# A mixture of experts behind a graph layer: the order of one step's four stages on TensorE and ScalarE turned round, and half of the last reads issued by ScalarE

## The chip, the cores and the metric

The kernel runs on one core of a Trainium2 chip. The metric is the device time of one execution in microseconds (us). Five engines work side by side, each through its own list of instructions in order: TensorE (PE, matmuls and transposes; its weight loads are PEld), VectorE (DVE), ScalarE (ACT), GpSimd (POOL) and SyncE (SP), which here does nothing but issue transfers. They wait for one another by semaphores. Sixteen DMA engines move data between memory (DRAM) and the on-chip buffers.

## The reference

The input is 3327 nodes with 128 features and a signed 3327x3327 matrix. A graph layer (a GRU cell over a graph sum, and one over three attention heads) is added to the nodes. Then comes a layer of 8 experts, and it is this part that the change touches:

```python
xn = (x - mu) * rsqrt(var + EPS) * gamma + beta
logits = einsum('bsd,de->bse', xn, Wr) + br
top_vals, top_idx = top_k(logits, 2)
w = softmax(top_vals)                      # two experts for each node
for e in range(8):
    h = gelu(einsum('bsd,dh->bsh', xn, W1[e]) + b1[e])     # 128 -> 256
    y_e = einsum('bsh,hd->bsd', h, W2[e]) + b2[e]          # 256 -> 128
    y = y + y_e * w_full[..., e, None]
```

The output is the nodes plus y.

## The kernel before, in words

The nodes are padded to 3328 = 26 tiles of 128. Everything up to about 870 us is the graph layer, the router and the sorting of rows, and the change does not touch it. At its end each node's normed row stands twice in `sorted_dram`, in the regions of its two experts, with its weight and the place where its result belongs. What follows has two parts.

**The batches.** 33 batches (`BATCHES`) of 256 rows (`SIDES` = 2 tiles of 128), each of one expert. Batch n passes through:

- SP: `weights_read(n)` and `rows_read(n)` (L543 to L554) bring the expert's weights and the 256 rows into one of 8 buffers (semaphore `b_in`). The first 8 are issued together, the later ones as `batch_y(n - 8)` is done.
- PE `batch_turned(n)` (L1881, matmuls on L1887): two 128x128 transposes into PSUM. ACT `batch_in(n)` (L887, L892): gamma and beta, PSUM to SBUF.
- PE `batch_hidden(n)` (L1890, L1896): W1, two products of 128x256. ACT `batch_gelu(n)` (L895, L901): two GELUs; the second releases `b_act`.
- PE `batch_down(n)` (L1901, L1907): W2, it waits for `b_act`. ACT `batch_kept(n)` (L905, L910): adds b2 and releases `b_kept`.
- PE `batch_back(n)` (L1911, L1917): two transposes back, after `b_kept`. DVE `batch_y(n)` (L1520, L1526): weighs the rows, into one of 4 buffers (`NY`); it waits until the buffer's earlier scatter has landed (`b_out`).
- POOL (L631 to L637): two indirect transfers, each 128 rows of y to their places in `y_dram` (L635).

An fp32 product of one weight tile stands in the trace as two matmul instructions, so L1896 and L1907 have four for a batch; the two transposes of L1887 or L1917 have two in all. The PE loop runs over steps n = -3 to 32 and in each step does batch n+3's first stage, n+2's second, n+1's third and n's fourth, **in this order: turned, hidden, down, back**. ACT's loop does `batch_in(n+3)`, `batch_gelu(n+2)`, `batch_kept(n+1)`. The order of these calls is the engine's order: an engine that waits for a semaphore holds all that stands behind it.

**The last sums.** When all scatters have landed (four waits on `b_out`), SP issues six reads of `y_dram` (L569), three pieces (`PIECES`: 6, 9 and 11 tiles) of each node's first and second result: `y_of[0]`, `y_of[1]`. DVE waits for both reads of a piece (`c_in[q]` at 32), adds both to the nodes (L1537), and SP writes the piece out (L573). SP's order is six reads, then three writes.

Of the kernel before, what the change touches and what calls it, by code (L numbers as in the profile page):

```python
# [29 lines left out]
NP = TILES * 128  # L30
# [18 lines left out]
SIDES = 2  # L49
BATCH = SIDES * 128  # L50
BATCHES = -(-2 * NP // BATCH) + E - 1
SPARES = BATCHES * BATCH
# [6 lines left out]
NY = 4  # L59
# [72 lines left out]
def graph_layer_kernel(nc, x, x_t, adj_rows, adj_cols, diag, ident_in, sum_parts_in, level_at_in,  # L132
# [9 lines left out]
    with ctx:  # L142
# [3 lines left out]
        def sem(name):  # L146
            return ctx.enter_context(nc.semaphore(name))
# [140 lines left out]
        y_of = [heads[:, k, :].rearrange("p (t f) -> p t f", f=H) for k in range(2)]  # L288
# [62 lines left out]
        b_out = [sem(f"b_out{k}") for k in range(NY)]  # L351
        c_in, c_out, o_done = [sem(f"c_in{k}") for k in range(3)], sem("c_out"), sem("o_done")
        PIECES = ((0, 6), (6, 15), (15, TILES))
# [61 lines left out]
        def _(sp):  # L415
# [93 lines left out]
            for c, (c0, w) in enumerate(CHUNKS):  # L509
                for third, (t0, t1) in enumerate(THIRDS):  # L510
                    n = 3 * c + third
# [53 lines left out]
            for k in range(NY):  # L565
                sp.wait_ge(b_out[k], 16 * SIDES * len(range(k, BATCHES, NY)))
            for q, (t0, t1) in enumerate(PIECES):
                for k in range(2):
                    sp.dma_start(y_of[k][:, t0:t1, :], y_dram[SPARES + k * NP + t0 * 128:SPARES + k * NP + t1 * 128, :]  # L569
                                 .rearrange("(t p) f -> p t f", p=128)).then_inc(c_in[q], 16)  # L570
            for q, (t0, t1) in enumerate(PIECES):
                sp.wait_ge(c_out, q + 1)
                sp.dma_start(out[t0 * 128:t1 * 128, :].rearrange("(t p) f -> p t f", p=128), x_kept[:, t0:t1, :])\  # L573
# [68 lines left out]
        def _(act):  # L642
# [11 lines left out]
            for q in range(-(-TILES // 4)):  # L654
                n = min(4, TILES - 4 * q) * 128
# [231 lines left out]
            def batch_in(n):  # L887

                act.wait_ge(b_turned, n + 1)
                if n >= 3:  # L890
                    act.wait_ge(b_hid, n - 2)
                nc.scalar.activation(turned[:, n % 3, :], bank[n % 2][:, 0:BATCH], ACT.Identity, bias=beta_sb,  # L892
                                     scale=gamma_sb).then_inc(b_input, 1)

            def batch_gelu(n):  # L895

                act.wait_ge(b_hid, n + 1)
                if n >= 3:
                    act.wait_ge(b_down, n - 2)
                for a in range(HALVES):  # L900
                    last = nc.scalar.activation(act_h[:, n % 3, a, :], bank[2 + n % 2][:, a * BATCH:(a + 1) * BATCH], ACT.Gelu,  # L901
                                                bias=b1_of[a][:, n % NX, :])
                last.then_inc(b_act, 1)

            def batch_kept(n):  # L905

                act.wait_ge(b_down, n + 1)
                if n >= 2:
                    act.wait_ge(b_back, n - 1)
                nc.scalar.activation(y_t[:, n % 2, :], bank[4 + n % 2][:, 0:BATCH], ACT.Identity, bias=b2_of[:, n % NX, :])\  # L910
                    .then_inc(b_kept, 1)

            act.wait_ge(tables_ready, 1)
            for n in range(-3, BATCHES):
                if n + 3 < BATCHES:
                    batch_in(n + 3)
                if 0 <= n + 2 < BATCHES:
                    batch_gelu(n + 2)
                if 0 <= n + 1 < BATCHES:
                    batch_kept(n + 1)  # L920


        @block.vector
# [620 lines left out]
        def _(pe):  # L1544
# [336 lines left out]
            def batch_turned(n):  # L1881

                pe.wait_ge(b_in[n % NX], 32 * (n // NX + 1))
                if n >= 2:
                    pe.wait_ge(b_input, n - 1)
                for k in range(SIDES):
                    last = nc.tensor.transpose(bank[n % 2][:, 128 * k:128 * (k + 1)], batch[:, n % NX, k, 0:H], ident[:, :])  # L1887
                last.then_inc(b_turned, 1)

            def batch_hidden(n):  # L1890

                pe.wait_ge(b_input, n + 1)
                if n >= 2:
                    pe.wait_ge(b_act, n - 1)
                for a in range(HALVES):
                    last = nc.tensor.matmul(bank[2 + n % 2][:, a * BATCH:(a + 1) * BATCH],  # L1896
                                            w1_of[a][:, n % NX, :], turned[:, n % 3, :],
                                            start=True, stop=True)
                last.then_inc(b_hid, 1)

            def batch_down(n):  # L1901

                pe.wait_ge(b_act, n + 1)
                if n >= 2:
                    pe.wait_ge(b_kept, n - 1)
                for a in range(HALVES):
                    last = nc.tensor.matmul(bank[4 + n % 2][:, 0:BATCH], w2_of[a][:, n % NX, :], act_h[:, n % 3, a, :],  # L1907
                                            start=a == 0, stop=a == HALVES - 1)
                last.then_inc(b_down, 1)

            def batch_back(n):  # L1911

                pe.wait_ge(b_kept, n + 1)
                if n >= 2:
                    pe.wait_ge(b_y, n - 1)
                for k in range(SIDES):
                    last = nc.tensor.transpose(bank[6 + n % 2][:, 128 * k:128 * (k + 1)], y_t[:, n % 2, 128 * k:128 * (k + 1)],  # L1917
                                               ident[:, :])
                last.then_inc(b_back, 1)

            for n in range(-3, BATCHES):
                if n + 3 < BATCHES:
                    batch_turned(n + 3)
                if 0 <= n + 2 < BATCHES:
                    batch_hidden(n + 2)
                if 0 <= n + 1 < BATCHES:
                    batch_down(n + 1)
                if n >= 0:
                    batch_back(n)


# [42 lines left out]
```

## Time and profile before

| | us |
|---|---|
| median of 3 runs | 1002.87 (1000.69 to 1006.1) |
| the profiled execution | 1000.35 |
| its span, first to last instruction | 998.6 |
| busy in the span: PE / DVE / ACT / POOL | 873.4 / 694.8 / 626.8 / 143.4 |
| first transpose of the batches to the last scatter's issue | 882.17 to 974.72 |
| first read of the last sums issued to the span's end | 976.97 to 998.6 |

The profile is of one execution. All times below are from the start of its span. A row of the timeline has start, duration, engine, line and operation; in brackets how long the engine was idle before and what ended that. The chain of waits is the path that ended last, followed back from the last instruction. Ends of matmuls are modelled (a row on L1896 shows 1.03 us, while the next matmul starts 0.86 us after it), starts are not.

### The profile page before, as it was taken

The numbers are of one execution on the slowest core, as the hardware profiler recorded it, in microseconds if no ns is written. First come the engines' busy times: TensorE is split into PE (matmuls) and PEld (weight loads), VectorE is DVE, ScalarE is ACT, GpSimd is POOL, SyncE is SP. The second block draws the span as 40 slices with busy tenths as digits, with TensorE's granted clock in tenths as the row PEclk, the third lists the DMA queues.
The fourth block names the chain that finished last, engine by engine and source line by source line (L and its number), as shares of the span: only waits on it lengthen the run. The fifth ranks groups of instructions, "written<-read, shape, count | busy, mean of one in ns | idle before, by whom it ended". The sixth has DMA issues, their size and how long they took to land.

```text
span 998.6 us, 10507 instructions
## 1 busy us (share of the span) xinstructions
PE 873.4 (87%) x2787; PEld 458.1 (46%) x2787; DVE 694.8 (70%) x1306; ACT 626.8 (63%) x918; POOL 143.4 (14%) x182
## 2 busy tenths in 40 slices
PE   5999999899699999999999999999988977069940
PEld 5734343356475434444444444444454444058830
DVE  6533333352599989999999999999858788612223
ACT  0655455611499879898998998989723233148820
POOL 0000000000000000001001001001000407727770
PEclk9999999999799999999999999999999998579975
DMA  9876766420059974646646445222040001268727
GB/s 282 278 270 233 255 236 228 147 88 17 9 176 309 330 176 121 167 111 190 169 117 160 122 122 143 84 87 103 1 142 1 27 6 46 72 170 222 220 72 213
DMA packets 115735, 147.81 MB, mean 148 GB/s; under 512 B 11488, under 2 KB 66562, under 8 KB 114786
## 3 DMA queue, kind: packets, MB, share of 16 engines
q1 hardware_dynamic: 111906, 139.38, 47.5%
q0 software_dynamic: 3776, 7.79, 2.2%
q8 instruction: 24, 0.39, 0.2%
q14 instruction: 29, 0.24, 0.1%
HBM read 123.61 MB, written 23.55 MB: 147 GB/s over the span
## 4 chain that ended last, share of the span: by engine, by line
PE 36%; issue 24%; DVE 19%; POOL 7%; DMA 5%; ACT 4%; DVEq 3%; SPq 1%; ACTq 0%; POOLq 0%
PE psum L1618 15%; DVE work L1257 9%; PE psum L1735 7%; POOL sorted_dram L628 4%; PE psum L1701 4%; POOL y_dram L635 4%; DVE big L1266 3%; DMA big<-adj_cols_dram 2%; DVEq L1257 2%; PE psum L1601 1%; ACT work L803 1%; PE psum L1559 1%; DMA h_t<-x_t_dram 1%; DMA y_dram<-rows 1%; PE psum L1896 1%
## 5 line engine op out<-in xcount | busy, mean ns | idle before, releaser
L1735 PE MATMUL psum<-big,h 128*128 128x512 f32 (+1 forms) x1092 | 445.4, 569 | 16.9 <-DVE big L1266 16.8
L1735 PEld LDWEIGHTS psum<-big,h 128*128 128x128 f32 x1092 | 206.7, 192 | 254.7 <-issue 178.9
L1266 DVE TENSOR_TENSOR big<-work,big 128x1536 f32<-128x1536 f32 (+1 forms) x182 | 299.2, 1644 | 9.2 <-ACT work L803 3.7
L801 ACT ACTIVATE work<-work,shift 128x1024 f32<-128x1024 f32 (+1 forms) x182 | 197.9, 1087 | 45.4 <-DVE work L1257 42.8
L1618 PE MATMUL psum<-big,h 128*128 128x512 f32 x312 | 146.3, 612 | 0.0
L1257 DVE TENSOR_SCALAR work<-rows,h 128x512 f32<-128x512 f32 x312 | 137.3, 483 | 2.9 <-POOLq L616 2.9
L803 ACT ACTIVATE work<-work,shift 128x512 f32<-128x512 f32 (+1 forms) x182 | 123.1, 676 | 0.0
L595 POOL TENSOR_SCALAR_AFFINE_SELECT big<-big 128x128 f32<-128x128 f32 x50 | 25.1, 502 | 639.5 <-DMA big<-adj_cols_dram 637.3
L797 ACT ACTIVATE work<-rows,h 128x512 f32<-128x512 f32 x156 | 110.2, 707 | 0.0
L1618 PEld LDWEIGHTS psum<-big,h 128*128 128x128 f32 x312 | 56.6, 191 | 68.6 <-issue 67.9
L675 ACT ACTIVATE work<-big 128x2048 bf16<-128x2048 f32 (+1 forms) x42 | 75.0, 1785 | 2.7
L1014 DVE TENSOR_SCALAR rows<-big 128x2048 fp8e4<-128x2048 f32 x36 | 42.5, 1224 | 48.9 <-POOLq L608 48.7
L635 POOL DMA_INDIRECT y_dram<-rows x66 | 63.8, 967 | 35.3 <-issue 18.0
L628 POOL DMA_INDIRECT sorted_dram<-big x52 | 52.3, 1006 | 100.2 <-ACT big L868 85.6
L1526 DVE TENSOR_SCALAR rows<-psum,rows 128x128 f32<-128x128 f32 x66 | 20.1, 347 | 62.9 <-DMA y_dram<-rows 38.1
L1001 DVE TENSOR_TENSOR work<-work,psum 32x512 f32<-32x512 f32 (+1 forms) x7 | 4.5, 637 | 57.5 <-ACT work L690 57.5
L1896 PE MATMUL psum<-work,rows 128*128 128x256 f32 x132 | 35.5, 394 | 0.0
L1701 PE MATMUL psum<-rows,work 128*126 128x512 fp8e4 (+1 forms) x168 | 35.0, 364 | 0.0
L901 ACT ACTIVATE work<-psum,rows 128x256 f32<-128x256 f32 x66 | 27.7, 471 | 11.2 <-PE psum L1896 11.2
L1907 PE MATMUL psum<-work,rows 128*128 128x256 f32 x132 | 34.0, 380 | 0.0
L892 ACT ACTIVATE work<-psum,u_parts 128x256 f32<-128x256 f32 x33 | 18.6, 565 | 22.1 <-PE psum L1887 22.0
L1887 PE MATMUL psum<-ident,rows 128*128 128x128 f32 x66 | 13.5, 287 | 19.1 <-DMA rows<-sorted_dram 19.1
(256 smaller groups left out, 763.3 us busy)
## 6 DMA issues: line engine op xcount, KB each, us to landing
big<-adj_cols_dram SPq DMA_DIRECT2D x30, 2048.0 KB, 8.1
sorted_dram<-zeros SPq DMA_DIRECT2D x15, 910.0 KB, 14.2
big<-adj_cols_dram SPq DMA_DIRECT2D x9, 1024.0 KB, 7.1
big<-adj_cols_dram SPq DMA_DIRECT2D x6, 1536.0 KB, 6.5
rows<-experts_dram SPq DMA_DIRECT2D x33, 257.5 KB, 3.1
rows<-stats_dram SPq DMA_DIRECT2D x1, 4608.0 KB, 26.9
rows<-sorted_dram SPq DMA_DIRECT2D x33, 130.0 KB, 2.9
rows<-stats_dram SPq DMA_DIRECT2D x1, 3840.0 KB, 21.0
```

The source lines that it names most:

```text
L628: nc.gpsimd.indirect_dma_start(out=sorted_dram[:, :], out_offset=bass.IndirectOffsetOnAxis(ap=slot_at[:, t, k:k + 1], axis=0), in_=rows_ou ...
L635: nc.gpsimd.indirect_dma_start(out=y_dram[:, :], out_offset=bass.IndirectOffsetOnAxis(ap=where_i[:, n, k:k + 1], axis=0), in_=y_sb[:, n % ...
L675: nc.scalar.activation(unused[:, 0:t1 - t0, 0:w], cols_of(c, t0, t1), ACT.Relu, scale=-1.0, accum_out=negative[:, NQ * c + g:NQ * c + g + ...
L797: nc.scalar.activation(place, row_of(c, LAST), ACT.Relu, bias=h[:, bass.ds(t, 1), H + SCORES + LAST]).then_inc(g_relu, 1)
L801: nc.scalar.activation(both, both, ACT.Exp, bias=shift[:, 0:1], scale=-1.0)
L803: nc.scalar.activation(place, place, ACT.Exp, bias=shift[:, 0:1], scale=-1.0).then_inc(g_e, 1)
L1257: last = nc.vector.tensor_scalar(wexp[:, (n + k) % SLOTS, i, 0:w], row_of(c, i), h[:, bass.ds(t, 1), H + i], 0.0, ALU.subtract, ALU.max)
L1266: nc.vector.tensor_tensor(wadj[:, k % 2, :, 0:w], wexp[:, (n + k) % SLOTS, :, 0:w], ring[:, bass.ds(place, 1), 0:w].broadcast_to([128, HEA ...
L1618: last = nc.tensor.matmul(bank[2 + c % 2][:, 0:w], h[:, t, 0:H], cols_of(c, t, t + 1).squeeze(1), start=t == 0, stop=t == TILES - 1)
L1701: last = nc.tensor.matmul(bank[6 + c % 2][0:STAT * LH, 0:w], weights[k][:, t - PREP * k, 0:STAT * LH], mask_of(t, c), start=t == 0, stop=t ...
L1735: done = nc.tensor.matmul(sums[i], h[:, t, 0:H], wadj[:, t % 2 if v == "plain" else 0, i, 0:w], start=t == 0, stop=t == TILES - 1)
L1896: last = nc.tensor.matmul(bank[2 + n % 2][:, a * BATCH:(a + 1) * BATCH], w1_of[a][:, n % NX, :], turned[:, n % 3, :], start=True, stop=True)
```

## The change

Three edits. In PE's loop the four calls of a step stand in the opposite order: back, down, hidden, turned. In ACT's loop the three calls stand in the opposite order: kept, gelu, in. Of the six reads of `y_dram` the three of `y_of[1]` leave SP's list and stand at the end of ACT's, behind the same four waits on `b_out`; SP keeps those of `y_of[0]`. No instruction is added but ACT's four waits.

```diff
@@ sync
             for q, (t0, t1) in enumerate(PIECES):
-                for k in range(2):
-                    sp.dma_start(y_of[k][:, t0:t1, :], y_dram[SPARES + k * NP + t0 * 128:SPARES + k * NP + t1 * 128, :]
-                                 .rearrange("(t p) f -> p t f", p=128)).then_inc(c_in[q], 16)
+                sp.dma_start(y_of[0][:, t0:t1, :], y_dram[SPARES + t0 * 128:SPARES + t1 * 128, :]
+                             .rearrange("(t p) f -> p t f", p=128)).then_inc(c_in[q], 16)
@@ scalar
             for n in range(-3, BATCHES):
+                if 0 <= n + 1 < BATCHES:
+                    batch_kept(n + 1)
+                if 0 <= n + 2 < BATCHES:
+                    batch_gelu(n + 2)
                 if n + 3 < BATCHES:
                     batch_in(n + 3)
-                if 0 <= n + 2 < BATCHES:
-                    batch_gelu(n + 2)
-                if 0 <= n + 1 < BATCHES:
-                    batch_kept(n + 1)
+
+            for k in range(NY):
+                act.wait_ge(b_out[k], 16 * SIDES * len(range(k, BATCHES, NY)))
+            for q, (t0, t1) in enumerate(PIECES):
+                nc.scalar.dma_start(y_of[1][:, t0:t1, :], y_dram[SPARES + NP + t0 * 128:SPARES + NP + t1 * 128, :]
+                                    .rearrange("(t p) f -> p t f", p=128)).then_inc(c_in[q], 16)
@@ tensor
             for n in range(-3, BATCHES):
+                if n >= 0:
+                    batch_back(n)
+                if 0 <= n + 1 < BATCHES:
+                    batch_down(n + 1)
+                if 0 <= n + 2 < BATCHES:
+                    batch_hidden(n + 2)
                 if n + 3 < BATCHES:
                     batch_turned(n + 3)
-                if 0 <= n + 2 < BATCHES:
-                    batch_hidden(n + 2)
-                if 0 <= n + 1 < BATCHES:
-                    batch_down(n + 1)
-                if n >= 0:
-                    batch_back(n)
```

## Rows read from the trace of the kernel before

**Rows 1.** Busy us by stretch (PE, PEld, DVE, ACT, POOL); granted clock, DMA share, GB/s.

```profile
890.00:900.00 10.00, 10.00 (x57) 8.82 (x57) 3.36 (x15) 8.68 (x20) 6.11 (x7) 1.00 0.60 159
...
960.00:970.00 10.00, 1.07 (x4) 0.47 (x4) 1.97 (x8) 0.00 (x0) 7.56 (x9) 0.62 0.15 51
```

**Rows 2.** The scatters: line L635 (min/median/max ns), then timeline, first and last.

```profile
L635 POOL DMA_INDIRECT y_dram<-rows x66: 963/967/977, 892.1 to 974.7; - x66
...
892.07 0.97 POOL L635 DMA_INDIRECT y_dram<-rows  x1 [15.46 <-DVE rows L1517]
...
974.72 0.97 POOL L635 DMA_INDIRECT y_dram<-rows  x1 [0.30 <-issue]
```

**Rows 3.** Chain of waits (start, us, what): batch 0's first product, then one step.

```profile
883.99 1.71 PE psum L1896 x4
...
892.60 0.22 PE psum L1917 x2
892.82 0.22 PE psum L1887 x2
893.03 0.86 PE psum L1896 x4
893.90 0.86 PE psum L1907 x4
```

**Rows 4.** Timeline, batch 0 on its way to its first scatter.

```profile
882.96 0.56 ACT L892 ACTIVATE work<-psum,u_parts 128x256 f32<-128x256 f32 x1 [18.83 <-PE psum L1887]
...
883.78 1.91 PE L1896 MATMUL psum<-work,rows 128*128 128x256 f32 x4
...
885.73 0.84 ACT L901 ACTIVATE work<-psum,rows 128x256 f32<-128x256 f32 x2 [1.14 <-PE psum L1896]
...
890.69 0.61 DVE L1526 TENSOR_SCALAR rows<-psum,rows 128x128 f32<-128x128 f32 x2 [8.38 <-PE psum L1917]
```

**Rows 5.** Timeline, the last batch: each stage waits for the one before it.

```profile
956.35 1.03 PE L1896 MATMUL psum<-work,rows 128*128 128x256 f32 x4
...
957.42 0.84 ACT L901 ACTIVATE work<-psum,rows 128x256 f32<-128x256 f32 x2 [0.61 <-PE psum L1896]
...
958.31 1.13 PE L1907 MATMUL psum<-work,rows 128*128 128x256 f32 x4
...
959.48 0.47 ACT L910 ACTIVATE work<-psum,rows 128x256 f32<-128x256 f32 x1 [0.72 <-PE psum L1907]
...
960.01 0.41 PE L1917 MATMUL psum<-ident,work 128*128 128x128 f32 x2 [0.57 <-ACT work L910]
```

**Rows 6.** The granted clock: four stretches (columns of rows 1), one row of PE's timeline.

```profile
882.00:887.30 5.30, 4.69 (x14) 3.53 (x15) 0.16 (x1) 2.42 (x5) 0.00 (x0) 0.50 0.48 120
887.30:892.00 4.70, 4.70 (x26) 4.12 (x25) 0.68 (x3) 3.84 (x9) 0.00 (x0) 1.00 0.25 63
...
820.00:825.00 5.00, 5.00 (x13) 3.08 (x13) 3.92 (x14) 1.75 (x6) 0.10 (x1) 0.50 0.00 0
...
958.00:960.00 2.00, 1.44 (x8) 0.85 (x7) 0.68 (x3) 1.21 (x3) 1.51 (x2) 1.00 0.19 66
...
818.58 1.45 PE L1846 MATMUL psum<-big,h 128*128 128x8 f32 x8 [3.31 <-DVE big L1438]
```

**Rows 7.** The last sums: timeline of SP and DVE, and chain of waits between.

```profile
976.97 7.90 SPq L569 DMA_DIRECT2D rows<-y_dram  x6
...
977.39 0.54 SPq L569
...
982.77 8.22 DMA rows<-y_dram
...
991.02 3.29 DVE L1537 TENSOR_TENSOR big<-big,rows 128x1408 f32<-128x1408 f32 x2 [2.16 <-DMA rows<-y_dram]
```

**Rows 8.** Stretches of the last reads, columns as in rows 1.

```profile
978.00:979.00 1.00, 0.00 (x0) 0.00 (x0) 0.00 (x0) 0.00 (x0) 0.00 (x0) 0.50 0.48 126
...
989.00:990.00 1.00, 0.00 (x0) 0.00 (x0) 0.00 (x0) 0.00 (x0) 0.00 (x0) 0.50 1.16 289
```

## The prediction

> **What bounds the kernel now.** I read the 40 slices first: only the last eighth of the span holds the code that changes. Then the batches in stretches of 10 us. From 890 to 900 PE is busy all the time and POOL is filling up; from 960 to 970 PE has almost nothing left and POOL is as busy as before [rows 1]. So the batches end with POOL, not with PE. The line of the scatters says by how much: 66 of them, the first at 892.07, the last at 974.72, so (974.72 - 892.07) / 65 = 1.27 us each, 2.54 us per batch, of which 0.97 is the transfer's own instruction and 0.30 the gap that follows each [rows 2]. POOL is never starved for longer than that gap. PE's step, in the chain of waits, is 0.22 + 0.22 + 0.86 + 0.86 = 2.17 us [rows 3]: 0.37 us per batch faster than POOL. That reserve of PE is what any change of order spends or keeps. After the last scatter come the reads, sums and writes, which run on the DMA engines [rows 7, 8].
>
> **The order on PE: what each distance is worth.** I count from the start of batch n's hidden stage, at the full clock. The last batch shows the serial chain with nothing beside it [rows 5]: hidden starts at 956.35, its GELU at 957.42 (1.07 later) and takes 0.84, and down starts at 958.31, which is 1.96 after hidden. This chain is the same in both orders; the question is how much other PE work lies between hidden(n) and down(n).
>
> Before: down(n) comes one step later, behind that step's hidden. Between the starts of hidden(n) and down(n) PE has hidden, down, back, turned and hidden again: 0.86 + 0.86 + 0.22 + 0.22 + 0.86 = 3.03. The chain needs 1.96, so it is covered with 1.07 to spare.
>
> After: in step n-2 PE does hidden(n) and then turned(n+1); step n-1 begins with back(n-1) and then down(n). Between the starts stand 0.86 + 0.22 + 0.22 = 1.30. The chain needs 1.96, so PE waits some 0.66 us in every step, before down; and hidden(n+1) stands behind that down. This closes a loop, hidden(n), GELU(n), down(n), hidden(n+1), that no buffer can loosen. Its length: 1.96 from hidden to down, and from down to the next hidden 0.86 [rows 3] and 0.10 for the first weight load, which no matmul hides after a wait (that down lasts 1.13, against the 1.03 of a hidden stage without a wait [rows 5]). Together **2.92 us per step**, against 2.17 before, and against POOL's 2.54. So PE's loop with ACT becomes the bound, and POOL idles about 0.38 us per batch.
>
> The other waits keep their cover. Back(n-1) needs kept(n-1): down's result reaches ACT 1.17 after down starts and takes 0.47 [rows 5], in all 1.64, and back comes 0.96 + 0.86 + 0.22 = 2.04 after down. ACT's turned order fits: kept is done 1.96 + 1.64 = 3.60 after hidden(n) and the next GELU's input is there at 2.92 + 1.07 = 3.99. In(n+1) starts behind GELU(n) and ends 1.07 + 0.84 + 0.56 = 2.47 after hidden(n) [rows 4, 5], 0.45 before hidden(n+1) wants it. The wait for a batch's rows now stands last in the step and holds back nothing late; 8 batches are in flight, and SP's loads follow batch_y, which gets slower. DVE's wait for a free buffer relaxes too.
>
> A page of the Trainium skill speaks of the 0.10: "TensorE: Matmul & The Clock Gate", "What happens when you issue a matmul", says that PE's queue can pull a weight load ahead of matmuls in flight. If it also passed the wait, the step would be 2.82 and the whole change 3 us cheaper. No row shows a load ahead of its stage's wait.
>
> **The start.** Batch 0 goes through with nothing late but itself. Hidden(0) stays at 883.78 and its GELU at 885.73, ending at 886.57 [rows 4]. Down(0), no longer behind hidden(1), starts at about 886.6 instead of 887.46. At the half clock a 0.86 stage takes 1.71 [rows 3]; the clock rose at about 887.3 [rows 6]. With half of down(0) at either clock hidden(1) starts at about 888.2. Back(0) comes 0.86 + 0.22 later, and y(0) after the transposes' own 0.41 [rows 5], at 889.7: 1.0 us before the 890.69 of rows 4. That head start would be worth 1.0 if POOL remained the bound.
>
> **The end of the batches.** Hidden(32) starts at 888.2 + 31 x 2.92 = 978.7. From there the chain of the last batch [rows 5]: down 1.96, kept 1.17 later and 0.47 long, the transposes 0.06 later, y 0.42 later and 0.61 long [rows 4], together 4.69. POOL's first scatter begins 0.2 to 0.8 after y (it began 892.07 where y ended at 891.30 [rows 2, 4]); I take 0.5, and the second 1.27 later. 978.7 + 4.7 + 0.5 + 1.3 = 985.2, against 974.72: **+10.5 us**. The bounds of the step carry the range: 31 x 0.10 = 3 less if the weight load hides; if the clock stays at half for one or two steps more, each costs 0.88 (hidden to GELU 1.95 [rows 4] instead of 1.07) and 0.85 (down 1.71 instead of 0.86), 1.73, so up to 3.5 more.
>
> **The last reads.** SP spends 7.90 us to issue six reads, the sixth going out at 982.77, though an early one takes 0.54 [rows 7]. Three on each engine, at 0.54 each, would all be out by 976.97 + 1.6 = 978.6. Read alone this promises 982.77 - 978.6 = 4 us. But the DMA engines are full behind the first microsecond (share 1.16 at 289 GB/s still from 989 to 990 [rows 8]), and the bytes stay the same: 2 x 26 x 128 rows of 512 bytes, 3.4 MB, are 11.8 us at 289 GB/s however they are queued; from the first packets after 978 that ends near the 991.02 at which the last piece is there [rows 7]. What can be gained is the ramp from 978 to 979, share 0.48, at most 0.5 us, and a queue that starts its first transfer sooner; what can be lost is the same if out writes, which SP can now issue at once, mix with the last read. No row shows an ACT transfer: I bound it at -4 to +1 and take **-0.5**, by the nearest row, the full share.
>
> The rule in the Trainium skill, "DMA: Bandwidth & Descriptors", section "Issuing engines are not separate DMA queues", is that transfers from all engines run on the same 16 and interleave. That speaks against the second half of this change, and the row at 989 agrees; by it alone the term is about 0.
>
> ACT's four waits stand last in its list, with only its three reads behind them.
>
> **The sum.** +10.5 - 0.5 = +10.0. Against the profiled execution's 1000.35 that is 1010.4; that execution is 2.5 under the median, whose own sum is 1012.9. The four times shown average 1002.5. I take **1012**.
>
> **Rivals.**
> 1. *POOL remains the bound (not slower).* The loop would have to close within 2.54 us. For it: PE has 0.37 per batch in reserve, and the oldest batch goes first. Against it: the 1.07 + 0.84 of rows 5 leave only 0.63 for down and its start, which takes 0.86 on PE alone. It decides at a step of 2.54: below it only the head start counts, -1.0 - 0.5 gives about 1001. Chance 0.10.
> 2. *The clock falls.* PE now idles about 0.5 us in each step. At the half clock the loop is 1.73 longer (0.88 and 0.85, above), 4.65, and the batches end 31 x 1.73 = 54 us later still, about 1066. Against it: with 1.44 busy of 2.00 the clock was 1.00 [rows 6], and the clock stood at half from 820 to 825 behind a pause of 3.31 us before 818.58, six times what the loop makes [rows 6]. For it: the start, at half clock, now has pauses too. Chance 0.05; one or two steps of it lie in the forecast's range.
> 3. *The loop holds but something gives part back*, the weight load passing the wait (-3) or the reads gaining their 4: 1008 to 1009. Chance 0.12.
> 4. *The order changes nothing*, as could be if PE had never waited in order: about 1002, chance 0.03.
>
> **How the numbers follow.** Forecast 0.70, 1009 to 1016 by itself. Rivals 1 and 4 lie within 0.5% (about what a measurement of this kernel can tell from no change), with a fifth of rival 1 below it. Range 1004 to 1020: it leaves out the clock rival and most of rivals 1 and 4. Faster 0.02, same 0.12, slower 0.86.
>
> **What would show it.** In the profile after: down's line with a wait of about 0.5 us for ACT's GELU in each step; hidden to hidden 2.9 us; POOL waiting for DVE about 33 times, some 0.4 us each; the clock at 1.00 from about 888; first y near 889.7, last scatter near 985; the last reads as long as before, at most 0.5 us shorter. Steps of 2.54 us with POOL's gaps at 0.30 would refute the loop. A loop much over 3 us, a clock below 1.00, or last reads that end 3 us sooner would move the time out of the forecast.

## The result, and the profile after

The changed kernel takes 1016.48 us (median of 4, 1013.49 to 1019.94) against 1004.49 us (median of 4) before: a ratio of 1.0144, 95% interval 1.0116 to 1.0173. A second comparison, taken later, gave 1012.75 against 1002.05, ratio 1.0109, interval 1.0084 to 1.0134. Twelve us slower and eleven: the change costs a little over 1%, and neither interval reaches 1.

The profiled execution of after took 1013.49 us, its span is 1011.7, 13.1 more than before. All of it lies in the two stretches that the change touches:

| us | before | after | difference |
|---|---|---|---|
| first transpose of the batches | 882.17 | 882.20 | 0.0 |
| from there to the last scatter's issue | 92.55 | 104.83 | +12.3 |
| last scatter to the first read | 2.25 | 2.25 | 0.0 |
| first read's issue to the span's end | 21.63 | 22.42 | +0.8 |

Busy time of PE, PEld, DVE, ACT and POOL in 10 us, then granted clock, DMA share and GB/s (the columns of rows 1):

```profile
890.00:900.00 10.00, 8.78 (x41) 6.67 (x39) 2.15 (x10) 5.86 (x14) 5.25 (x6) 0.91 0.46 136
...
950.00:960.00 10.00, 8.50 (x42) 6.90 (x43) 2.28 (x11) 5.76 (x14) 6.35 (x8) 1.00 0.63 183
960.00:970.00 10.00, 8.51 (x44) 6.67 (x42) 2.03 (x9) 6.14 (x15) 6.73 (x8) 1.00 0.42 120
970.00:980.00 10.00, 8.04 (x39) 6.49 (x40) 2.71 (x12) 6.18 (x15) 6.49 (x7) 1.00 0.14 46
```

Where PE was at 10.00 of 10 and then ran dry by 960 [rows 1], it now does 8.0 to 8.5 up to 980, and POOL, 7.56 before, is down to 6.4 to 6.7. No engine is full. The scatters' line in after (L634; idle time before it by releaser), and its first and last in the timeline:

```profile
L634 POOL DMA_INDIRECT y_dram<-rows x66: 962/966/975, 892.7 to 987.0; - x66
...
  DVE rows L1522: 35.3, 29
  issue: 12.0, 37
...
892.66 0.97 POOL L634 DMA_INDIRECT y_dram<-rows  x1 [15.79 <-DVE rows L1522]
...
987.03 0.96 POOL L634 DMA_INDIRECT y_dram<-rows  x1 [0.30 <-issue]
```

POOL now waits for DVE 29 times. The first wait is the 15.8 us before batch 0; the other 28 come to 19.5 us, 0.70 each, where rows 2 had only its own gaps of 0.30. One step of PE with ACT's GELU in after's timeline (L1901 hidden, L900 GELU, L1912 down):

```profile
977.29 1.03 PE L1901 MATMUL psum<-work,rows 128*128 128x256 f32 x4
...
978.36 0.84 ACT L900 ACTIVATE work<-psum,rows 128x256 f32<-128x256 f32 x2 [0.39 <-PE psum L1901]
...
979.25 0.73 PEld L1912 LDWEIGHTS psum<-work,rows 128*128 128x128 f32 x4 [0.73 <-ACT work L900]
979.25 1.13 PE L1912 MATMUL psum<-work,rows 128*128 128x256 f32 x4 [0.49 <-ACT work L900]
...
980.22 1.03 PE L1901 MATMUL psum<-work,rows 128*128 128x256 f32 x4
```

Hidden to GELU 1.07, to down 0.89, to the next hidden 0.97: 2.93 us. From the third hidden on all 30 steps are 2.92 or 2.93. PE stands 0.49 us before each down; before, this wait did not exist.

The start, in after's timeline, and the granted clock by stretch:

```profile
883.60 2.07 PE L1901 MATMUL psum<-work,rows 128*128 128x256 f32 x4 [0.71 <-ACT work L891]
...
885.72 0.84 ACT L900 ACTIVATE work<-psum,rows 128x256 f32<-128x256 f32 x2 [2.16 <-PE psum L1901]
...
886.61 2.08 PE L1912 MATMUL psum<-work,rows 128*128 128x256 f32 x4 [0.50 <-ACT work L900]
...
888.47 1.91 PE L1901 MATMUL psum<-work,rows 128*128 128x256 f32 x4
...
891.28 0.61 DVE L1531 TENSOR_SCALAR rows<-psum,rows 128x128 f32<-128x128 f32 x2 [8.94 <-PE psum L1922]
...
892.53 1.03 PE L1901 MATMUL psum<-work,rows 128*128 128x256 f32 x4
...
888.00:891.00 3.00, 3.00 (x10) 2.24 (x8) 0.00 (x0) 1.05 (x3) 0.00 (x0) 0.50 0.33 87
891.00:892.00 1.00, 0.93 (x4) 0.62 (x3) 0.68 (x3) 0.72 (x2) 0.00 (x0) 0.58 0.00 0
892.00:893.00 1.00, 1.00 (x7) 0.87 (x6) 0.00 (x0) 0.27 (x1) 0.34 (x1) 1.00 0.00 0
```

Batch 0's down starts at 886.61, sooner than the 887.46 at which it stood before. But the clock, which rose at 887.3 in rows 6, stays at half to 891.8, so the first two steps take 4.87 and 4.06 us, and the first y comes at 891.28, 0.6 later than in rows 4 and not 1.0 sooner.

The tail of after: the reads on both queues, DVE's last piece, and the second, third and fourth microsecond behind the first read's issue; last, the second and third of them in before.

```profile
989.28 1.83 SPq L568 DMA_DIRECT2D rows<-y_dram  x3
989.28 2.94 ACTq L924 DMA_DIRECT2D rows<-y_dram  x3
...
1004.11 3.28 DVE L1542 TENSOR_TENSOR big<-big,rows 128x1408 f32<-128x1408 f32 x2 [1.56 <-DMA rows<-y_dram]
...
990.28:991.28 1.00, 0.00 (x0) 0.00 (x0) 0.00 (x0) 0.00 (x0) 0.00 (x0) 0.50 0.37 93
991.28:992.28 1.00, 0.00 (x0) 0.00 (x0) 0.00 (x0) 0.00 (x0) 0.00 (x0) 0.50 0.94 284
992.28:993.28 1.00, 0.00 (x0) 0.00 (x0) 0.00 (x0) 0.00 (x0) 0.00 (x0) 0.50 1.16 331
...
977.97:978.97 1.00, 0.00 (x0) 0.00 (x0) 0.00 (x0) 0.00 (x0) 0.00 (x0) 0.50 0.45 119
978.97:979.97 1.00, 0.00 (x0) 0.00 (x0) 0.00 (x0) 0.00 (x0) 0.00 (x0) 0.50 1.11 330
```

All six reads are issued within 2.94 us instead of 7.90 [rows 7], and the last piece is there 14.83 us after the first issue instead of 14.05. The saved time to issue bought nothing.

### The profile page after: what moved, and what is told of

It is laid out like the page before. It is cut to its first block, busy times and chain, and to the rows that moved or that the text cites. A ratio compares the mean times of both kernels' runs of the same rounds, so it can differ in the third digit from the quotient of the medians.

```text
span 1011.7 us, 10509 instructions
## 1 busy us (share of the span) xinstructions
PE 881.7 (87%) x2787; PEld 459.4 (45%) x2787; DVE 694.1 (69%) x1306; ACT 624.1 (62%) x918; POOL 143.3 (14%) x182
## 4 chain that ended last, share of the span: by engine, by line
PE 39%; issue 24%; DVE 19%; DMA 5%; ACT 5%; POOL 4%; DVEq 3%; SPq 0%; ACTq 0%; POOLq 0%
PE psum L1623 15%; DVE work L1262 9%; PE psum L1740 6%; POOL sorted_dram L627 4%; PE psum L1706 4%; PE psum L1912 4%; DVE big L1271 3%; PE psum L1901 3%; DMA big<-adj_cols_dram 2%; DVEq L1262 2%; ACT work L900 2%; DMA rows<-y_dram 1%; PE psum L1606 1%; PE psum L1564 1%; ACT work L802 1%
## 5 line engine op out<-in xcount | busy, mean ns | idle before, releaser
L634 POOL DMA_INDIRECT y_dram<-rows x66 | 63.8, 966 | 47.4 <-DVE rows L1522 35.3
L1912 PE MATMUL psum<-work,rows 128*128 128x256 f32 x132 | 38.5, 415 | 16.0 <-ACT work L900 16.0
L900 ACT ACTIVATE work<-psum,rows 128x256 f32<-128x256 f32 x66 | 27.7, 470 | 15.5 <-PE psum L1901 15.5
L1901 PE MATMUL psum<-work,rows 128*128 128x256 f32 x132 | 35.8, 396 | 0.7 <-ACT work L891 0.7
L1912 PEld LDWEIGHTS psum<-work,rows 128*128 128x128 f32 x132 | 23.1, 195 | 26.1 <-ACT work L900 24.2
L909 ACT ACTIVATE work<-psum,rows 128x256 f32<-128x256 f32 x33 | 15.6, 473 | 26.9 <-PE psum L1912 26.9
```

## The experiments

The place of the first transpose moved between 881 and 894 us from one profile to another, in kernels that are the same up to there. (In the two kernels with matmuls ahead of the batches, told of below, it stood at 891 and 897.) So I compare profiles by the length of the batches, first transpose to last scatter's issue, and of the tail, first read's issue to the last piece at DVE:

| kernel | batches, us | steady step of PE, us | tail, us |
|---|---|---|---|
| before | 92.55 | 2.17, later held by POOL | 14.05 |
| after | 104.83 | 2.92 | 14.83 |
| after, second comparison | 104.58 | 2.92 | 14.85 |
| order alone | 104.63 | 2.92 | 14.42 |
| reads alone | 93.17 | 2.17, later held by POOL | 14.87 |
| one batch more between hidden and down | 95.06 | 2.52 | 14.11 |
| GELU released in halves | 94.52 | 2.62 | 14.54 |
| PE's order alone | 144.38 | 4.13 | 14.12 |
| ACT's order alone | 131.37 | 3.74 | 14.18 |
| before, half the scatters | 77.21 | 2.17 | 14.74 |
| order alone, half the scatters | 103.95 | 2.92 | 14.11 |
| 13 matmuls ahead of the batches | 111.57 | 2.17, with pauses | 14.22 |
| reads alone, writes held | 114.39 | 2.17, with pauses | 14.12 |
| 13 matmuls, pieces turned round | 109.96 | 2.17, with pauses | 14.42 |

**The two parts of the change, each alone.** First the order, with all six reads on SP as before (the diff is that of the change without its hunk of SP and the reads at the end of ACT's):

> The turned order on PE and ACT alone; all six reads stay with SP. Loop theory: hidden to hidden 2.92 us, first y at about 891.3 and last scatter at about 987.0, as in the changed kernel; the tail from the first read's issue to the last piece 14.05 us, as before. Time: the changed kernel's less 0.8 us. Rival (the second queue is what costs): hidden to hidden near 2.2, last scatter near 975, time as before.

Measured: 1013.82 against 1002.44 us, ratio 1.0108 (1.008 to 1.0136); batches 104.63 with steps of 2.92. The whole loss is the order's.

Then the reads, with both engines in the order of before:

```diff
-                for k in range(2):
-                    sp.dma_start(y_of[k][:, t0:t1, :], ...
+                sp.dma_start(y_of[0][:, t0:t1, :], ...
+            # at the end of ACT's list, behind the waits on b_out
+                nc.scalar.dma_start(y_of[1][:, t0:t1, :], ...
```

> The reads on two queues alone; PE and ACT in the order of before. If the changed kernel's longer tail comes from the two queues: first read's issue to DVE's last piece 14.8 us instead of 14.05, time 0.8 us over the kernel before, last scatter unchanged near 974.7. If it only came by chance or from the later place in time: 14.05 and no difference. By my prediction (a gain of 0.5): 13.5.

Measured: ratio 1.000 (0.9981 to 1.002). The tail was 14.87 us, as in both profiles of after (14.83, 14.85), where SP alone had 14.05 to 14.54 in seven kernels with the same reads and pieces (and 14.11 and 14.74 in the two that read the input rows). So the tail is some 0.6 us longer, not far outside what it varies by; in the time this can't be seen. My predicted gain of 0.5 is not there.

**The distance between hidden and down.** Oldest batch first is kept, but hidden and turned run one batch further ahead:

```diff
-            for n in range(-3, BATCHES):
+            for n in range(-4, BATCHES):
                 ...
-                    batch_hidden(n + 2)
-                if n + 3 < BATCHES:
-                    batch_turned(n + 3)
+                    batch_hidden(n + 3)
+                if n + 4 < BATCHES:
+                    batch_turned(n + 4)
```

(and batch_gelu and batch_in alike)

> Oldest batch first as in the changed kernel, but hidden (with its GELU) and turned (with its input step) run one batch further ahead: a step does back(n), down(n+1), hidden(n+3), turned(n+4). Between hidden(n) and down(n) PE then has 3.46 us of work instead of 1.30. Reads with SP. Distance theory: PE no longer waits for the GELU, steps of 2.17 where POOL lets them, POOL at 2.54 is the bound again, last scatter within 2 us of 974.7 (first y some 1.3 us later), time within 0.5% of before. Rival (oldest first costs by itself, through the waits or the clock, however far apart the stages): 2.9 us steps remain, last scatter near 987.

Measured: 1002.94 against 1002.44, ratio 1.0009 (0.9982 to 1.0036); batches 95.06. The loss is gone with the order turned all the same: it was the distance, not the order as such. The step, though, is not 2.17 but 2.52, in every one of the last 29. The timeline of this kernel (L1896 hidden, L901 GELU, L892 the input step):

```profile
920.78 1.13 PE L1896 MATMUL psum<-work,rows 128*128 128x256 f32 x4
...
921.95 0.84 ACT L901 ACTIVATE work<-psum,rows 128x256 f32<-128x256 f32 x2 [0.74 <-PE psum L1896]
...
922.68 0.57 ACT L892 ACTIVATE work<-psum,u_parts 128x256 f32<-128x256 f32 x1
...
923.30 0.73 PEld L1896 LDWEIGHTS psum<-work,rows 128*128 128x128 f32 x4 [0.48 <-ACT work L892]
923.30 1.13 PE L1896 MATMUL psum<-work,rows 128*128 128x256 f32 x4
```

A second loop lies under the first: the input step stands behind the GELU on ACT, and the next hidden waits for it. 1.17 + 0.73 + 0.62 = 2.52. It is as long as POOL's 2.54, and only so does it cost nothing. The 3.46 us of work that I counted between hidden and down do cover the GELU, as PE no longer waits before down, but they did not set the step. Most of the 2.5 us by which the batches are longer than before's is the start: the first scatter comes 12.06 us after the first transpose, against 9.90.

**The loop shortened.** In the turned order the GELU's release comes in halves (hidden's wait on the same semaphore is counted in halves too):

```diff
-                last.then_inc(b_act, 1)                      # after both GELUs
+                                         ...).then_inc(b_act, 1)   # after each
 ...
-                pe.wait_ge(b_act, n + 1)
                 for a in range(HALVES):
+                    pe.wait_ge(b_act, HALVES * n + a + 1)
```

> The turned order, reads with SP, but the GELU's release is given in halves: down's first product starts after the first of the two GELUs, 0.42 us sooner. Loop theory: the loop shortens by what is taken from it, 2.92 to 2.5 us, which is POOL's 2.54, last scatter near 976 and time 11 us under the turned order alone. Rival (the loss is in steps further on, as the wait of hidden for its input): the wait moves and the step stays over 2.8.

Measured: 1004.53 against 1002.44, ratio 1.0018 (0.9997 to 1.004); step 2.62, batches 94.52, 10.1 less than the order alone. In its timeline (L1895 hidden, L1906 down):

```profile
919.96 1.03 PE L1895 MATMUL psum<-work,rows 128*128 128x256 f32 x4
...
921.02 0.84 ACT L901 ACTIVATE work<-psum,rows 128x256 f32<-128x256 f32 x2 [0.39 <-PE psum L1895]
...
921.64 1.10 PE L1906 MATMUL psum<-work,rows 128*128 128x256 f32 x4 [0.22 <-ACT work L901]
...
922.58 1.03 PE L1895 MATMUL psum<-work,rows 128*128 128x256 f32 x4
```

Down starts 0.62 after the first GELU does, 0.47 for the GELU and 0.15 until PE runs. I had counted 0.42 saved and got 0.30 (2.92 to 2.62). Of the 0.12 that is missing, 0.05 is a single GELU's length, 0.47 where half of the pair's 0.84 is 0.42. Most of the rest stands on PE: between the GELU's end at 921.49 and the first weight load at 921.61 PE now executes a wait instruction of its own, 0.05 us long. In the changed kernel nothing stands there, and the load starts 0.05 after ACT's end. (The line of these waits, one for each batch from the third on:)

```profile
L1905 PEldq EVENT_SEMAPHORE  x31: 51/51/51, 895.3 to 974.0; - x31
```

The step follows the length of the chain, and the loop theory stands.

**One engine's order alone.** The hunk of PE alone, then that of ACT alone:

> PE's order turned, ACT's as before (in, gelu, kept), reads with SP. Queue theory: ACT now does in(n+3) ahead of gelu(n+2), and PE's turned(n+3) stands last, so the GELU starts 1.88 us after hidden instead of 1.07, and back(n+1), first on PE, waits for kept at 3.25; then 0.22 and 0.86: a step of 4.36 us, time some 45 us over the turned order on both, about 1058. If only PE's order matters: 2.92 and 1014.

> ACT's order turned, PE's as before (turned, hidden, down, back), reads with SP. Queue theory: kept(n+1) heads ACT's step and waits for down, which is third on PE; GELU and in follow only then, and hidden of the next step waits for in at 3.02 after down's start: step 3.07 + 0.96 = 4.03 us, time about 1048. If only PE's order matters: as before, about 1002.

Measured: 1063.18 and 1050.72 us, on a chip where the kernel before took 1028.89, once each, so only their profiles are used: steps of 4.13 and 3.74, batches of 144.4 and 131.4 us, with the clock at 1.00 (PE's alone, 17.76 busy of 30 us):

```profile
930.00:960.00 30.00, 17.76 (x90) 14.18 (x90) 5.02 (x23) 11.59 (x28) 13.63 (x15) 1.00 0.47 126
```

Both are far worse than both together: each engine's order has to fit the other's. The steps came 0.23 and 0.29 shorter than forecast. PE's order alone, timeline of ACT and PE:

```profile
931.55 0.56 ACT L892 ACTIVATE work<-psum,u_parts 128x256 f32<-128x256 f32 x1 [2.48 <-PE psum L1887]
932.01 0.83 ACT L901 ACTIVATE work<-psum,rows 128x256 f32<-128x256 f32 x2
932.72 0.48 ACT L910 ACTIVATE work<-psum,rows 128x256 f32<-128x256 f32 x1
933.25 0.20 PEld L1917 LDWEIGHTS psum<-ident,work 128*128 128x128 f32 x2 [1.98 <-ACT work L910]
```

ACT's next instruction starts 0.10 to 0.12 us before the one ahead of it ends (932.01 against 932.11, 932.72 against 932.84), which the forecasts did not count. Two such joints in a step make 0.22 us: nearly all of the 0.23 in this kernel, and most of the 0.29 in the other.

**What bounds each order.** The second scatter of each batch is left out, and the last reads take the input rows in place of the results, which are thus not added (DVE and SP wait for half as many landings):

```diff
-                for k in range(SIDES):
+                for k in range(1):
                     nc.gpsimd.indirect_dma_start(out=y_dram[:, :], ...
 ...
-                ... y_dram[SPARES + k * NP + t0 * 128:...]
+                ... x[t0 * 128:t1 * 128, :]
```

> The order of before with the second of each batch's two scatters left out, and the last six reads taken from the input rows instead of the results (same sizes); the results are thus not added. If POOL is the bound before: PE's 2.17 us step shows in full, last scatter some 79 us after the first transpose instead of 92.6, time 13 us less, about 989. If something else paces the batches (the landing of scatters, DVE): less than 5 us gained.

> The turned order, reads with SP, with the same scatters left out and the same reads replaced as in the run on the order of before. If the loop of PE and ACT is the bound: the steps stay at 2.92 us and only the last backlog of POOL goes, about 2 us, time about 1012, last scatter about 103 us after the first transpose. If POOL still counts in the turned order: over 5 us gained.

Measured: 992.75 and 1021.64 us, once each, on the chip where the kernel before took 1028.89. Batches 77.21 us in the order of before, 15.3 less than with all scatters; 103.95 in the turned order, 0.7 less. Both differences are against profiles from a faster chip, since there is no profile of the kernel before from this one. The forecast of 79 and 103 us for the batches held. The time did not follow: against the kernel before on the same chip the first kernel is 36 us faster, not 13, which is taken up again below. In the order of before PE is full to the end once POOL is relieved:

```profile
950.00:960.00 10.00, 10.00 (x56) 8.72 (x55) 3.00 (x14) 8.36 (x19) 4.15 (x5) 1.00 0.55 149
```

The run takes away the landing of half the scatters together with POOL's time for them. That it is POOL's own pace and not the landing which holds the kernel before is read from what stood ahead of its 66 scatters, in 59 cases nothing but POOL's own gap:

```profile
  issue: 18.0, 59
```

POOL bounds the batches before and not after; in the turned order's loop the second scatter hides almost whole.

**The start, the tail, and a version against both.** Thirteen matmuls on PE, into a bank that nobody reads, fill its wait for the first rows:

```diff
+            pe.wait_ge(tables_ready, 1)
+            for _ in range(13):
+                nc.tensor.matmul(bank[7][:, :], ident[:, :], h_t[:, 0:CHUNK], start=True, stop=True)
```

> The kernel before with 13 matmuls of 128x512 on PE between the tables (about 868.4) and the first batch's rows (882.2), into a PSUM bank that nothing reads; order and reads as before. If the slow start is the half clock: clock 1.00 when the first transposes start, hidden(0) to its GELU 1.07 instead of 1.95, first y some 2.5 us sooner after the first transpose, and as POOL is the bound there, last scatter 90 us after the first transpose instead of 92.6; time 2.5 us less. If the matmuls run past the rows' arrival they cost what they overlap.

SP's writes, on the kernel with its reads on two queues, held back until the reads are done:

```diff
+            sp.wait_ge(c_in[2], 32)
             for q, (t0, t1) in enumerate(PIECES):
                 sp.wait_ge(c_out, q + 1)
```

> Reads on two queues, order of before, and SP's writes held until the last piece's reads have landed. If the two queues' longer tail comes from writes that overtake the reads: first read's issue to DVE's last piece 13.1 us (3.41 MB alone) instead of 14.8, the writes of pieces 0 and 1 hidden beside DVE's last sums, time 1 to 2 us under before. If it comes from the start of the reads on two queues: the last piece is there 14.5 us after the issue, and no gain.

And the thirteen matmuls with the pieces turned round:

```diff
-        PIECES = ((0, 6), (6, 15), (15, TILES))
+        PIECES = ((0, 11), (11, 20), (20, TILES))
```

> A version meant to beat both: the kernel before, the same 13 matmuls ahead of the batches, and the last sums in pieces of 11, 9 and 6 tiles instead of 6, 9 and 11. The last sums of DVE then take 1.95 instead of 3.28 us and the last write is smaller; last read's landing as before. 2.5 + 2 us less, about 0.45% under before. If the last write's time does not depend on its size, 2.5 + 1.3.

These three ran on a chip where the kernel before takes 1030.14 us. Measured: 1030.33, ratio 1.0003 (0.9982 to 1.0024); 1031.65, ratio 1.0023 (1.0006 to 1.004); 1029.16, ratio 0.9985 (0.9965 to 1.0004). No version was shown to be faster than the kernel before.

The second interval lies wholly above 1: two queues with the writes held are 0.2% slower than the kernel before, where 1 to 2 us less had been expected.

What the profiles say of the parts: with the thirteen matmuls the clock is 1.00 at the first transpose, and the first scatter comes 7.93 us after it in both kernels that have them, against 9.90 before. These 2.0 us stand in the profiles and do not show in the time. On this chip the batches took 110 to 114 us and not 92.6, so what the head start is worth where POOL is the bound was not measured. The time goes in pauses like this one, in the kernel with the thirteen matmuls and everything else as before (stretches, then timeline: L1900 hidden, L901 GELU, L1911 down, L1921 back, and the clock behind the pause):

```profile
904.00:905.00 1.00, 0.79 (x4) 0.36 (x2) 0.00 (x0) 0.00 (x0) 0.69 (x2) 1.00 0.14 50
905.00:906.00 1.00, 0.00 (x0) 0.00 (x0) 0.00 (x0) 0.18 (x1) 0.94 (x1) 1.00 0.57 131
906.00:907.00 1.00, 0.29 (x1) 0.29 (x2) 0.00 (x0) 0.65 (x2) 0.00 (x0) 0.91 0.70 260
...
901.81 0.81 PE L1900 MATMUL psum<-work,rows 128*128 128x256 f32 x3
...
903.32 0.38 PE L1921 MATMUL psum<-ident,work 128*128 128x128 f32 x2
...
905.82 0.84 ACT L901 ACTIVATE work<-psum,rows 128x256 f32<-128x256 f32 x2 [2.33 <-PE psum L1900]
906.71 1.99 PE L1911 MATMUL psum<-work,rows 128*128 128x256 f32 x4 [1.92 <-issue]
...
907.33 0.61 DVE L1526 TENSOR_SCALAR rows<-psum,rows 128x128 f32<-128x128 f32 x2 [5.08 <-remote]
...
906.80:910.20 3.40, 3.40 (x11) 2.75 (x12) 1.35 (x6) 2.58 (x6) 1.20 (x2) 0.50 0.48 124
```

PE, DVE and ACT stand still for about 2 us, while POOL only finishes what it has. Nine steps of PE in this kernel take 3.9 to 5.6 us, where its work is 2.17. Part of the standing still is the pipeline's own: PE's down waits for the GELU that starts at 905.82. But that GELU had its input from a hidden stage that ended at 902.62, and DVE's multiplication at 907.33 had its input from transposes that ended at 903.70. Nothing in the profile says what held them. The cause stays open. It need not be the chip alone. The other slow chip gave four profiles (one engine's order alone, half the scatters), and none of them has such pauses: their steps are even. In all four POOL's work (2.54 us a batch, or 1.27 with half the scatters) is less than PE's step, and in the three kernels here it is more. If the kernel before met the pauses on that chip too and its half left them out, the 36 us above would be explained; no profile shows it. The run of the changed kernel that was to see whether the turned order meets them too got a chip without them:

> The changed kernel itself once more, against the kernel before on whatever chip the call gets; the calls so far found the kernel before at 1002 us on one and at 1029 to 1030 on others. Loop theory where before takes about 1002: steps of 2.92 us, last scatter 104.8 us after the first transpose, 12 us more, ratio 1.012. Where before takes about 1030, its batches are paced by pauses in which PE, ACT and DVE stop together and not by POOL (109 to 114 us from first transpose to last scatter in the runs there); if the longer step leaves room for those pauses, the changed kernel's batches take 105 to 110 us there too and the ratio is 1.00 to 1.005; if the pauses come on top of the loop, 118 us or more and 1.012 again.

Measured: 1012.75 against 1002.05, as told above; steps of 2.92, last scatter 104.6 us after the first transpose. It confirms the first half of the expectation. The second half, what the change does on a chip with the pauses, was not tried; the nearest is the turned order with half the scatters on the other slow chip, with 103.95 us and no pauses.

The held writes put the last piece at DVE 14.12 us after the first issue instead of 14.87. That is within what one queue gave, so the longer tail of two queues comes from SP's writes mixing with ACT's reads, as far as one profile with the writes held can show it. ACT's last read, issue to landing, without and with the writes held:

```profile
rows<-y_dram ACTq DMA_DIRECT2D x1, 704.0 KB, 13.7
...
rows<-y_dram ACTq DMA_DIRECT2D x1, 704.0 KB, 13.0
```

The end of the span came 21.97 us after the first read against 22.47, which is again what one queue gives. The expected 13.1 did not come. The turned pieces shortened the tail as far as the span's end to 19.6 us, against 21.6 to 22.2 with SP's reads and the old pieces: the forecast 2 us are there.

## Why the prediction was right, and where it was off

Forecast 1012, range 1004 to 1020; measured 1016.48 and 1012.75. The profile gives the better account: forecast +10.0, measured +13.1. Of the 3.1 missing, 1.8 lies in the batches and 1.3 in the last reads. All the errors went the same way, so the hit owes nothing to errors that cancel. Step by step:

- **The loop** of hidden, GELU, down, hidden: forecast 2.92, measured 2.92. The row that carried it was the last batch of the trace of before [rows 5], the one place where nothing lay beside the chain. That the loop is what costs is shown: shortened by 0.30 it gives back 10.1 us, some 9 of them as 30 steps of 0.30, with the distance restored it vanishes, and halving POOL's work leaves it as it is.
- **POOL as the bound before**: right, 15.3 us less with half its scatters. That it goes idle after: right. The forecast was 33 waits of 0.4 us; the 28 waits behind the first average 0.70, since the 0.30 that POOL would have paused anyway counts in each.
- **The start**: wrong by sign. I let the clock rise at 887.3, when it had risen before, though PE now pauses at the start. It rose at 891.8, 9.6 us after the first transpose instead of 5.1. Pauses at the start and a late clock go together in the other profiles: with this order and this release of the GELU it rose 8.9 to 10.5 us after the first transpose (four profiles), with the order of before 5.0 to 6.5 us after (four). With the GELU released in halves, where PE's second pause was 0.14 and not 0.50, it rose 6.5 us after, and with ACT's order alone turned, where PE did not pause at all, 3.5 us after. The term was to be H(1) = 888.2 and then steps of 2.92; it was 888.47 and one step of 4.06. That is 1.4 us of the 1.8 by which the batches came out longer than the +10.5; I had it as a bound of the range (1.73 for each step at half clock) and should have taken one step of it as the value.
- **The end of the batches**: 6.81 us from hidden(32) to the last scatter, against 6.5.
- **The last reads**: forecast -0.5, measured +0.4 to +0.8 in the profiles, nothing measurable in the time. The argument that full DMA engines leave nothing to win was right (the share is 1.16 three microseconds after the issue); the sign of the rest was wrong. I named the writes that mix with the reads as a possible loss, and that is what came: with them held the tail is as long as with one queue. I took the gain of the ramp instead, and on two queues the ramp is slower, not faster: 0.37 and 0.94 in the second and third microsecond, where one queue had 0.45 and 1.11.
- **The weight load ahead of its wait** (rival 3): no. L1912's loads start at 979.25, with the matmul, behind ACT's release, and the line has ACT ahead of all 33.
- **The clock in the loop** (rival 2): 1.00 from 891.8 to the end of the batches, with PE pausing 0.49 us in each step; with PE's order alone turned, 17.76 us busy of 30, it stayed at 1.00 too. Where a pause was longer it did fall: to half for 3.4 us behind the 1.92 us before 906.71 in the kernel with the thirteen matmuls.
- **A loop I passed over**: GELU, input step, hidden. I had its length (2.47, "0.45 before hidden wants it") and used it only as cover. It is the next bound, at 2.52.

## What to carry to other kernels

In a software pipeline over in-order engines, count for each pair of dependent stages how much other work the queue holds between them, against the time of the chain between them through the other engine; turning this step's order round took two stages of 0.86 us out of that distance, 3.03 to 1.30, and the chain needs 1.96. Read the chain's length where the pipeline drains, since there nothing hides it, and list every loop through two queues, not only the first that binds. Two engines' orders belong together: one turned alone cost the batches 52 or 39 us where both cost 12. And where transfers already fill the DMA engines, a second queue for them saves issue time only, and it let the writes mix with the last reads here.

## What the runs showed of the hardware that I had not expected

- Where PE paused 0.5 to 0.7 us in its first microseconds, its clock rose 8.9 to 10.5 us after its first transpose instead of 5.0 to 6.5. Pauses of 0.49 us in each step did not lower it later: it stayed at 1.00 for over 90 us. That the early pauses are the cause is read from the profiles of several orders; no run changed them alone.
- ACT's back-to-back instructions start 0.10 to 0.12 us before the one ahead ends. What PE does behind one of them has no such lead: its weight load starts 0.05 us behind the end (979.25 behind 979.20 in after), or 0.11 where PE first executes a wait of its own.
- Two of the chips used ran the unchanged kernel at 1029 to 1030 us, where the other comparisons had it at 1002 to 1004. On one of the two the batches showed pauses in which PE, DVE and ACT stopped together for some 2 us; on the other, four kernels that leave POOL time to spare ran without them.
